# A hybrid transformer block on one core: the new sequence's causal layer moved ahead of the old one's last gated layer, and the order of all steps replaced

## What is computed

```
x = x + attn_a(norm(x))     # layer 0: causal attention, 16 heads of 16, rotary Q and K
x = x + ffn(norm(x))        # layer 1: gated layer
x = x + attn_b(norm(x))     # layer 2: 16 heads of 64, with a bias for relative position
x = x + ffn(norm(x))        # layer 3: the gated layer again, with the same weights
```

## Time and profile before

| | us |
|---|---|
| median of 3 runs | 2064.11 |
| lowest and highest | 2063.27, 2064.46 |
| the profiled execution | 2061.41 |
| its span | 2059.7 |

### The profile page before, as it was taken

One profiled execution on the slowest core, in us unless ns is written; L12 is line 12 of the kernel. 1 busy time (PEld: TensorE's weight loads), 2 busy tenths in 40 slices (PEclk: granted clock), 3 DMA queues, 4 the chain that ended last, 5 costly groups with the idle time before them and its releaser, 6 DMA issues.

```text
span 2059.7 us, 42179 instructions
## 1 busy us (share of the span) xinstructions
PE 1988.9 (97%) x16097; PEld 1282.8 (62%) x16097; DVE 1516.3 (74%) x4803; ACT 1152.8 (56%) x2578; POOL 692.5 (34%) x879
## 2 busy tenths in 40 slices
PE   8999999999999999999999999999999999999998
PEld 6676666655666556765566655665566655675667
DVE  8977654967868767778778687686876967857446
ACT  2535764756637475374755657466573756627742
POOL 5323232343414433234423343234341343413320
PEclk9999999999999999999999999999999999999999
DMA  4001121120102211121111211012110120102200
GB/s 166 2 1 35 52 77 45 61 98 17 63 16 73 73 35 44 34 80 55 35 37 52 83 42 45 19 59 83 35 63 2 60 90 17 63 16 70 70 1 22
DMA packets 31079, 102.46 MB, mean 50 GB/s; under 512 B 3104, under 2 KB 11424, under 8 KB 30752
## 3 DMA queue, kind: packets, MB, share of 16 engines
q1 hardware_dynamic: 30880, 99.76, 14.6%
HBM read 95.56 MB, written 4.19 MB: 48 GB/s over the span
## 4 chain that ended last, share of the span: by engine, by line
PE 76%; DVE 12%; ACT 5%; POOL 3%; issue 2%; DVEq 0%; POOLq 0%
PE ps L960 18%; PE ps L1709 11%; PE ps L1691 11%; PE ps L1699 10%; PE ps L1470 9%; ACT PTc L1198 3%; PE ps L1553 3%; PE ps L1658 3%; PE ps L1646 3%; PE ps L1567 3%; DVE ps L1325 2%; PE ps L1529 2%; DVE peaks L1399 2%; DVE probs L1416 2%; PE ps L1624 1%
## 5 line engine op out<-in xcount | busy, mean ns | idle before, releaser
L1133 POOL TENSOR_SCALAR probs<-probs,rtotal 128x512 f32<-128x512 f32 x512 | 345.9, 695 | 513.2 <-DVE rtotal L1425 512.3
L1225 ACT ACTIVATE probs<-probs,peak 128x512 f32<-128x512 f32 x512 | 365.3, 715 | 134.2 <-DVE peak L1421 133.3
L1416 DVE CUSTOM_DVE_ANT_0 probs<-ps,band 128x512 f32<-128x512 f32 x512 | 332.7, 687 | 60.6 <-PE ps L1691 60.2
L1234 ACT ACTIVATE PT<-ps 128x512 f32<-128x512 f32 x512 | 261.5, 620 | 52.5 <-PE ps L1699 52.1
L1699 PE MATMUL ps<-ident,probs 128*128 128x128 f32 x2048 | 245.3, 274 | 3.6 <-DVE peaks L1399 2.2
L1325 DVE CUSTOM_DVE_ANT_0 ps<-ps,later 128x512 f32<-128x512 f32 (+3 forms) x512 | 232.6, 526 | 20.3 <-PE ps L1529 20.0
L1691 PE MATMUL ps<-KT,QT 64*128 64x512 f32 x1024 | 243.8, 607 | 0.0
L1699 PEld LDWEIGHTS ps<-ident,probs 128*128 128x128 f32 x2048 | 225.2, 141 | 29.2 <-POOL probs L1133 12.0
L1709 PE MATMUL ps<-PT,Vb 128*64 128x512 f32 x1024 | 237.0, 600 | 0.0
L960 PE MATMUL ps<-xnT,wb 128*128 128x512 f32 x512 | 233.4, 600 | 0.6 <-ACT xnT L1158 0.6
L1198 ACT ACTIVATE PTc<-ps 128x384 f32<-128x384 f32 (+1 forms) x384 | 168.2, 549 | 42.4 <-PE ps L1553 41.4
(11 more groups left out here) (156 smaller groups left out, 3343.0 us busy)
## 6 DMA issues: line engine op xcount, KB each, us to landing
band<-in_band SPq DMA_DIRECT2D x64, 896.0 KB, 4.6
wb<-in_w_b SPq DMA_DIRECT2D x64, 384.0 KB, 3.1
x<-in_x SPq DMA_DIRECT2D x16, 256.0 KB, 3.0
out<-x SPq DMA_DIRECT2D x16, 256.0 KB, 2.2
cos<-in_cos SPq DMA_DIRECT2D x8, 256.0 KB, 2.7
sin<-in_sin SPq DMA_DIRECT2D x8, 256.0 KB, 2.9
wob<-in_wo_b SPq DMA_DIRECT2D x1, 1024.0 KB, 8.6
wqk<-in_wqk_a SPq DMA_DIRECT2D x1, 512.0 KB, 5.8
```

Source lines behind the costliest of these rows:

```text
L1133: last = g.tensor_scalar(unit, unit, rtotal[:, r % 8, e:e + 1], 1.0, ALU.mult, ALU.mult)
L1225: last = a.activation(unit, unit, ACT.Exp, bias=peak[:, r % 8, e:e + 1], accum_out=total[:, r % 8, e:e + 1])
L1234: a.activation(PT[:, k % 2, e, :, tile_of(q)], bank(now, name).rearrange("p (k n) -> p k n", k=NT), ACT.Copy).then_inc(act_read, 1)
L1416: v.tensor_tensor_reduce(out=probs[:, r % ROWS_HELD, e, :], in0=bank(now, name), in1=band[:, k % 2, e, lo:lo + T], scale=1.0, scalar=-3e38 ...
```

## The change

The change has five parts.

1. `whole()` adds the causal layer of s + 1 first, ahead of the gated layer 3 of s - 1, which must now follow it; the gated layer 1 of s + 1 comes after both. The causal layer no longer follows the strand's last layer as a whole.
2. `causal_steps` says instead what of the gated layer 1 of sequence s - 1 it must follow: `c_ln` after `f_part`, `c_xt` after the four `f_p2` and `f_vb` 0, and `c_q`, `c_k`, `c_v` after `f_vb` 1. So `c_xt` may now come ahead of `f_o` and `f_y`. ACT waits at `c_xt` until `f_vb` 0 has been scaled.
3. xnTc moves from column 9728 to column 7168 of its memory, where the second half of Dq lies. `c_dq` 1 therefore follows both `c_k` and both `c_v`, and DVE waits at it until PE has finished them. A wait of ACT at `c_p2` 0, 2 for `c_q` and `c_k` falls away, as does the need of `c_p2` 0, 2 to follow the products.
4. The rotary tables are loaded at `f_vb` 1 of layer 1 of the sequence before, in place of layer 3 of the sequence before that.
5. CYCLE becomes 2820 and every number of PLACE is new.

```diff
-CYCLE = 2805
+CYCLE = 2820
 PLACE = {
...
-    ("cycle", "b_xt"): [3459],
-    ("cycle", "c_dq"): [-7637, 1401],
-    ("cycle", "c_k"): [-10624, 1724],
-    ("cycle", "c_p1"): [1698, 1865, -39885, 1776, 1819, 1844, -51740, 2050, 2246, -12312, 2137, 2296],
-    ("cycle", "c_q"): [-12764, -3766],
-    ("cycle", "c_v"): [1840, 1756],
-    ("cycle", "c_xt"): [-12844],
-    ("cycle", "f_o"): [3383],
-    ("cycle", "f_y"): [3437, 2898],
-    ("last", "b_y"): [40475, -3170, 7469, -3229],
-    ("last2", "f_o"): [39842],
-    ("last2", "f_y"): [41504, 5562],
...
+    ("cycle", "b_xt"): [609],
+    ("cycle", "c_dq"): [-2169, -3162],
+    ("cycle", "c_k"): [-2212, -2224],
+    ("cycle", "c_p1"): [-2080, -1998, -3161, -1868, -1816, -2966, -1572, -1565, -1478, -1519, -1488, -1381],
+    ("cycle", "c_q"): [-2237, -1956],
+    ("cycle", "c_v"): [-1844, -1846],
+    ("cycle", "c_xt"): [-2314],
+    ("cycle", "f_o"): [580],
+    ("cycle", "f_y"): [594, 404],
+    ("last", "b_y"): [26897, 1344, 1337, -547],
+    ("last2", "f_o"): [23815],
+    ("last2", "f_y"): [25507, 21560],
...
     late = [Step("f_y", s - 3, 3, 1)] if s >= 3 else []
-    turned = [Step("f_vb", s - 2, 3, 1)] if s >= 2 else []
-    out = [(c("ln"), late, [Step("f_part", s - 2, 3)] if s >= 2 else []), (c("xt"), [c("ln")], side)]
+    cleared = [Step("f_p2", s - 1, 1, i) for i in range(4)] + [Step("f_vb", s - 1, 1, 0)] if s >= 2 else []
+    turned = [Step("f_vb", s - 1, 1, 1)] if s >= 2 else []
+    out = [(c("ln"), late, [Step("f_part", s - 1, 1)] if s >= 2 else []), (c("xt"), [c("ln")], side + cleared)]
     for i in range(2):
-        out += [(c("q", i), [c("xt")] + turned, []), (c("k", i), [c("xt")] + turned, []), (c("dq", i), [c("q", i)], []),
+        out += [(c("q", i), [c("xt")] + turned, []), (c("k", i), [c("xt")] + turned, []),
+                (c("dq", i), [c("q", i)], [c(w, j) for w in ("k", "v") for j in range(2)] * i),
...
-    out += [(c("v", i), [c("xt")], []) for i in range(2)]
-    lent = {0: [c("xq", 0), c("xq", 1)], 1: [c(w, i) for w in ("q", "k") for i in range(2)], 2: [c(w, i) for w in ("q", "k", "v") for i in range(2)]}
+    out += [(c("v", i), [c("xt")], turned) for i in range(2)]
+    lent = {0: [c("xq", 0), c("xq", 1)], 1: [c(w, i) for w in ("q", "k") for i in range(2)]}
...
         if s > 0:
-            gone = add(ffn_steps(s - 1, 3), left, side)
-            side = gone
+            turned = []
             if s + 1 < B:
-                side = add(ffn_steps(s + 1, 1), add(causal_steps(s + 1, side), [], []), [])
+                turned = add(causal_steps(s + 1, []), [], [])
+            side = add(ffn_steps(s - 1, 3), left, turned + side)
+            if s + 1 < B:
+                side = add(ffn_steps(s + 1, 1), turned, side)
                 entered.append(side)
...
-                          part("xnTc", 6144 + 7 * T, [P, NC, T]), part("cos", 8192, [P, T]), part("sin", 8704, [P, T]), i, part("Vx", 11776, [P, 2, VALUES]) if i else Vx, rsums[i])
+                          part("xnTc", 7168, [P, NC, T]), part("cos", 8192, [P, T]), part("sin", 8704, [P, T]), i, part("Vx", 11776, [P, 2, VALUES]) if i else Vx, rsums[i])
...
-                        if kind == "f_vb" and l == 3 and n == 1 and s + 2 < B:
+                        if kind == "f_vb" and l == 1 and n == 1 and 1 <= s < B - 1:
                             sp.wait_ge(heads_done, plan.after("heads", now, now))
-                            load_rope(sp, s + 2)
+                            load_rope(sp, s + 1)
...
+                        if kind == "c_xt" and s >= 2:
+                            act.wait_ge(scaled_done, plan.after("scaled", Step("f_vb", s - 1, 1, 0), now))
...
-                            if n == 0 and q == 2:
-                                for what in ("c_q", "c_k"):
-                                    at_least(act, dve_full, plan.unit(Step(what, s, l, 1), now))
...
+                            if kind == "c_dq" and n == 1:
+                                for i in range(2):
+                                    at_least(dve, act_full, plan.unit(Step("c_v", s, l, i), now))
+                                    at_least(dve, dve_full, plan.unit(Step("c_k", s, l, i), now))
```

More of the change, by code:

```diff
@@ new lines @@
+    ("first", "b_v"): [-2706, 1228, 1970, 1812, 2321, 2856, 988, 1270],
+    ("first", "b_val"): [2007, 27, 1676, 1666, 2213, 1414, 1997, 1666, 3262, 431, 2178, 2263, 2495, 2269, 1123, 614,
+        3138, -6227, 2762, -410, 2760, 1787, 270, 3274, -16949, -1244, -10276, 3499, 2480, 3317, 3228, -6266],
+    ("first", "b_xt"): [3220],
+    ("first", "b_y"): [3978, 3253, 3083, 2641],
+    ("first0", "c_dk"): [0, 320],
+    ("first0", "c_dq"): [-61, 193],
+    ("first0", "c_hk"): [-1464, 365],
+    ("first0", "c_hm"): [-642, -564],
@@ new lines @@
+    ("first0", "c_k"): [-336, 69],
+    ("first0", "c_ln"): [-5084],
+    ("first0", "c_m"): [377, -39],
+    ("first0", "c_p1"): [352, -641, 282, 291, 233, -878, 262, 379, -1568, 261, 409, 303],
+    ("first0", "c_p2"): [245, 386, 471, 523, -1463, 412, 189, 502, 569, 63, -546, 334],
+    ("first0", "c_q"): [-455, 70],
+    ("first0", "c_rq"): [-10, 259],
+    ("first0", "c_v"): [-472, 298],
+    ("first0", "c_va"): [423, 552, 89, 794, 194, 327],
+    ("first0", "c_vb"): [502, 589, 313, 806, 556, -1327],
@@ new lines @@
+    ("first0", "c_xq"): [58, 340],
+    ("first0", "c_xt"): [97],
+    ("first0", "c_y"): [817, -322],
+    ("first0", "f_gate"): [556],
+    ("first0", "f_gather"): [1185],
+    ("first0", "f_hk"): [-3236],
+    ("first0", "f_hm"): [-90, 594],
+    ("first0", "f_k"): [192],
+    ("first0", "f_ln"): [873],
+    ("first0", "f_m"): [1240, 1290],
+    ("first0", "f_o"): [1443],
+    ("first0", "f_p1"): [1218, 1204, 1249, 1232],
+    ("first0", "f_p2"): [-961, 1263, 190, 1317],
+    ("first0", "f_part"): [131],
@@ new lines @@
+    ("first0", "f_q"): [-3296],
+    ("first0", "f_rank"): [1007],
+    ("first0", "f_row"): [921],
+    ("first0", "f_rq"): [-124],
+    ("first0", "f_spread"): [1272],
+    ("first0", "f_v"): [313],
+    ("first0", "f_va"): [1308, 1356],
+    ("first0", "f_vb"): [937, 906],
+    ("first0", "f_xq"): [606],
+    ("first0", "f_y"): [524, 820],
+    ("first1", "c_dk"): [242, 555],
+    ("first1", "c_dq"): [326, 266],
+    ("first1", "c_hk"): [234, 351],
+    ("first1", "c_hm"): [836, 333],
+    ("first1", "c_k"): [-310, 547],
@@ new lines @@
+    ("first1", "c_ln"): [-4250],
+    ("first1", "c_m"): [-2195, 1204],
+    ("first1", "c_p1"): [557, -303, 614, 87, 800, 68, 813, 825, 928, 916, 1135, 929],
+    ("first1", "c_p2"): [907, 964, 411, 606, -913, 928, -70, 134, 191, 1050, 1340, 1280],
+    ("first1", "c_q"): [194, 463],
+    ("first1", "c_rq"): [364, 767],
+    ("first1", "c_v"): [315, 268],
+    ("first1", "c_va"): [1002, 1203, 908, 1226, 1155, 1264],
+    ("first1", "c_vb"): [1215, 843, 1122, 1377, -54, 1224],
+    ("first1", "c_xq"): [534, 713],
@@ L434 @@
+    ("last2", "f_part"): [17827],
+    ("last2", "f_q"): [19593],
+    ("last2", "f_rank"): [20251],
+    ("last2", "f_row"): [20060],
+    ("last2", "f_rq"): [17889],
+    ("last2", "f_spread"): [17457],
+    ("last2", "f_v"): [20714],
+    ("last2", "f_va"): [21597, 22051],
+    ("last2", "f_vb"): [18925, 8164],
+    ("last2", "f_xq"): [20585],
+    ("last2", "f_y"): [25507, 21560],
 }
```

361 lines of the change are left out of this document (143 added, 218 removed).

## The result

The changed kernel takes 2030.5 us (median of 4 runs, 2030.32 to 2036.46) against 2063.7 us before: a ratio of 0.9845, with a 95% interval of 0.983 to 0.9859. The forecast was 2056.8 us with a range of 2038 to 2078 us.

What follows compares the result with a forecast made beforehand. It took PE's work as the bound in the cycles, leaving only idle time, fillers and tile-shape losses to move. Terms of -6.6, -2.7 and +2.0 us took 2064.1 to 2056.8 us; range 2038 to 2078 us.

Steps and rivals of the forecast that it cites:

- The cycle's idle time spread over `c_p1` and `c_p2`: Six cycles, PE's remaining waits, such as for ACT's exponential: taken as 0, bounds -20 and +12 us.
- that for POOL: `c_p1` in each cycle, PE's wait for POOL's low half of K: -2.7 us, bounds 0 and -5.4 us.
- The stub at `c_xt`: Six fillers and 0.30 us idle between `c_xt` and `c_q`, to be covered by `f_o`: -6.6 us over six cycles.
- rival A: Cycles: the strand gets slack and the new order closes half of idle time and padding; 2038 us, chance 0.17.
- The start: 7 to 180 us: keeps its chain and DVE work, so 0, with 5 us allowed each way.
- The end: Tail after the last `b_y`: `f_y` of sequence 6 moves from it into a full stretch, +2.0 us.
- the tables' load: Rotary tables loaded later, before `c_q`: taken as 0, with +6 us kept for the range.
- Rival D: Cycles: DVE held at `c_dq` 1 waiting for PE's products, slower; 2082 us, chance 0.11.
- Rival C: `c_p1` to `c_vb` beside the biased layer: ten more runs of narrow tiles a cycle, slower; 2078 us, chance 0.15.
- the test of a cycle of 238.5 us: Sign that the forecast is right: a cycle, believed to be 240 us, takes 238.5 us after the change.

Runs made afterwards that it cites:

- e4: Kernel before with its old layers and rules; only the numbers of PLACE found anew by a ten-minute search; 2045.0 us.
- e8: Kernel before with its old layers and rules; numbers of PLACE after a further 25 minutes of search; 2032.2 us.
- e1: Changed kernel, given table, with the overlap undone: `c_xt` must follow the last `f_y` of the gated layer before it; 2044.1 us.
- e2: Changed kernel with the steps up to the first `b_xt` nearly in the order of the kernel before; 2042.5 us.
- e6: Changed kernel without the overlap (`c_xt` behind the last `f_y`), with PLACE fitted by a ten-minute search; 2022.3 us.
- e5: Changed kernel's layers and rules with the numbers of PLACE found anew by a ten-minute search from its given table; 2017.5 us.
- e9: Changed kernel's layers and rules with PLACE searched 40 minutes more, after an earlier ten-minute search; 2009.0 us.
- e3: Changed kernel without any of its 527 fillers, all else as it is; 2054.1 us.
- e10: The new layers with the longest-searched table (2009.0 us), with more fillers in start and end; 2016.3 us.

## Why the prediction was wrong

**The cycle's idle time spread over `c_p1` and `c_p2` was the term that failed.** The prediction took 0 for it, with the reason that the causal layer still has a biased layer beside it. In the four cycles the waits for ACT's exponential fell by 6.0 us and that for POOL by all of its 3.6 us, of which I had counted half. The stub at `c_xt` went as predicted: its wait of 0.3 us and its 0.8 us of fillers a cycle are gone, and `f_o` stands between. A further 0.8 us of fillers in each cycle, which the sum had not priced at all, went too. Together the cycles and the stretches next to them gave 23.1 us of the 31.2, where the sum had 9.3 us.

**The reason was wrong more than the number.** I argued from the mix of work, which the change does not alter. And rival A's "against" took the old order for one improved as far as it goes. That premise is false: e4 and e8 have the old layers, and search alone took POOL's wait away in both and brought the exponential's waits from 8.3 to 1.1 us in e8. In e1 both stay low without the overlap. So these waits belonged to the table, or to table and layers together, and not to the overlap. I priced rival A at 2038 us and gave it 0.17. Idle time and fillers in four cycles fell from 36.3 to 20.1 us, a little less than half, so its amount is what came in the cycles, though its mechanism, a strand that starts earlier, is shown for the stub alone. Its time was 7.5 us too long: it had nothing for the start (6.9 us), 2 us the wrong way for the end (which gave 1.2), some 5 us too much in the cycles, and 2.4 us lie between the medians and the profiled executions.

**The start was taken as 0 within 5 us.** It gave 6.9 us. The 12.2 us of idle time and 50.5 us of fillers stood in the prediction; I read DVE's 146.0 of 173 us as a bound, though it left 27 us. That an order alone can win this is shown by e4, which has the old layers and rules and gained 6.7 us there.

**The end had the wrong sign.** The sum had +2.0 us for moving `f_y` of sequence 6 ahead of the last `b_y`. That step moved as said, but the end shortened by 1.2 us and the stretch of sequences 6 and 7 by 2.2 us.

**The other terms.** Between 600 and 1560 us DVE's own waits name none at `c_dq` 1, and PE's none for the tables' load. Rival D did not occur in the changed kernel's cycles, but e2's order showed its wait in the start, at 2.7 us. Rival C had the wrong sign, 64 runs for 69. The cycle's length, 240 us, was misread (247.1), so the test of a cycle of 238.5 us was meaningless. The scale of 11.75 numbers a microsecond would have been 11.4, but the error is larger than that: the numbers are priorities and not times. The prediction read 13.4 us between `c_q` 0 and the first `c_p1` and the trace has 25.0; it read 33 us from `c_q` 0 to `c_dq` 1 and the trace has 47.1 (572.75 to 619.87). So POOL's wait was gone whole and not by half.

**What caused the gain.** The stub is the overlap's: 1.1 to 1.2 us a cycle, there in e6 and e8 and gone in the changed kernel, e5 and e9. The waits for POOL and the exponential and the length of the start can be won by the table alone, as e4 and e8 show. With a table fitted to each, the new layers' cycle came out 2 to 5 us shorter than the old ones' (e4 and e5, e8 and e9). That exceeds the spread of 1.3 and 1.8 us between searches of one set, but narrowly after the long ones, and how it divides between the order of the layers, the moved xnTc and the search is not shown. Nearly all of the changed kernel's 33 us were within the old layers' reach: e8 got 31 us by search alone. What stays open is how short either cycle can get.

## What to carry to other kernels

When a change comes with a new order found by search, price the order as a term of its own: the idle time and padding in each stage are what it can win, in the start and the end as much as in the cycles. To judge a change of structure in such a kernel, fit the order to both structures with the same effort, and more than once: with a table made for the other side, e1 put the overlap at 13.6 us where the fitted pair gave 4.7 us, and two searches of one structure differed by 1.3 to 1.8 us a cycle. And measure a cycle from a step to the same step, not by windows of a guessed length.

## What was not expected of the hardware

Filler matmuls in the gaps were worth 23.6 us (e3): without them the mean granted clock was 0.81 from 7 to 180 us and 0.82 in the last 68 us, with 0.99 and 1.00 in between. More of them was no better: 12.8 us more in the start left the clock at 0.99 and cost 5.4 us there (e10).
